# Attention and two mixture-of-experts layers: GpSimd splits the negated score maxima, weight loads placed between, and their transpose comes one score pair later

## The reference, cut to what matters

```python
x = x + _L0_ffn_ref(_L0_cond_ref(x, cond_1024, mask, ...), ...)
x = x + _L1_ffn_ref(_L1_cond_ref(x, cond_1024, L1_cond_weight), ...)
```

```python
scores = jnp.einsum('bhqd,bhkd->bhqk', q, k) / jnp.sqrt(jnp.float32(HDIM))
scores = jnp.where(causal[None, None], scores, jnp.float32(MASK_OUT))
scores = scores + mask
attn = jax.nn.softmax(scores, axis=-1)
out = jnp.einsum('bhqk,bhkd->bhqd', attn, v)
```

## Time and profile before

| What | us |
|---|---|
| three runs: lowest, median, highest | 392.42, 395.8, 398.46 |
| the profiled execution, its own time | 392.82 |
| its span, first to last instruction | 391.1 |
| mean granted clock of PE in it, share of full speed | 0.871 |
| attention stage in it (scores of group 0 to the last exponentials' use) | 35 to 156 |

### The profile page before, as it was taken

The page is one execution under the profiler, slowest core; times in us unless marked ns, Lnnn a source line. Parts: engine busy times, 40 slices in busy tenths (PEclk is TensorE's granted clock), DMA queues, the critical chain, the costliest instruction groups (busy, mean ns, idle before and its releaser), DMA issues.

```text
span 391.1 us, 8159 instructions
## 1 busy us (share of the span) xinstructions
PE 294.7 (75%) x2751; PEld 196.2 (50%) x2765; DVE 270.9 (69%) x717; ACT 184.4 (47%) x406; POOL 122.4 (31%) x161
## 2 busy tenths in 40 slices
PE   2747679999986798638988999999970748499800
PEld 1445334444433432327987867666640725277700
DVE  4396868888986563676997777777748686468503
ACT  7333056666752177502764445554445406167502
POOL 8304000101100057017055322222221077127760
PEclk9975689999998989655999999999995859789965
DMA  5679972345421024731278411110003011322114
GB/s 169 241 195 263 345 314 69 94 148 153 142 70 54 0 84 115 235 108 49 76 228 254 142 35 29 36 36 22 16 22 115 0 44 52 93 54 57 42 44 162
DMA packets 23238, 43.07 MB, mean 110 GB/s; under 512 B 4173, under 2 KB 13612, under 8 KB 23070
## 3 DMA queue, kind: packets, MB, share of 16 engines
q0 software_dynamic: 8336, 26.47, 20.3%
q1 hardware_dynamic: 13758, 13.38, 13.0%
q10 hardware_dynamic: 1104, 2.70, 1.8%
HBM read 26.99 MB, written 15.30 MB: 108 GB/s over the span
## 4 chain that ended last, share of the span: by engine, by line
PE 43%; DVE 20%; POOL 12%; DMA 9%; issue 9%; ACT 4%; SPq 1%; ACTq 1%; POOLq 0%; DVEq 0%
PE pair L1150 9%; POOL x_slots L685 6%; POOL y_rows L738 6%; DVE mA L1472 4%; PE bank L1171 4%; PE pair L979 3%; PE bank L1021 3%; PE pair L1120 3%; PE bank L999 3%; DMA xg<-x_slots 2%; DMA back<-y_rows 2%; PE bank L1160 2%; PE pair L981 2%; PE bank L1013 2%; DVE w_sb L1411 1%
## 5 line engine op out<-in xcount | busy, mean ns | idle before, releaser
L810 ACT ACTIVATE p_ring<-bank 128x512 f32<-128x512 f32 (+1 forms) x88 | 45.5, 566 | 33.7 <-PE bank L1002 33.5
L668 POOL DMA_DIRECT2D w_ring<-in_L_ffn_W_dram x24 | 18.4, 770 | 135.1 <-DVE w_sb L1411 116.3
L1472 DVE TENSOR_REDUCE mA<-pair 128x2 f32<-128x256 f32 (+3 forms) x64 | 50.8, 820 | 12.3 <-PE pair L981 12.1
L821 ACT ACTIVATE h<-pair,cols 128x128 f32<-128x128 f32 x108 | 30.8, 374 | 53.4 <-PE pair L1120 44.8
L685 POOL DMA_INDIRECT x_slots<-sent,slot x32 | 33.1, 1034 | 33.5 <-DVE slot L1721 17.2
L1150 PE MATMUL pair<-w_sb,h 128*128 x180 | 41.3, 379 | 0.0
L722 POOL DMA_INDIRECT y_rows<-y_sb,id_now x19 | 21.1, 1109 | 57.3 <-DVE y_sb L1616 42.6
L979 PE MATMUL pair<-kr,qr 128*128 128x128 bf16 (+3 forms) x122 | 33.7, 331 | 6.3 <-DVE mA L1472 5.4
L999 PE MATMUL bank<-qr,kr 128*128 128x384 bf16 (+3 forms) x120 | 31.2, 306 | 1.4 <-ACT p_ring L810 0.9
L1411 DVE SCALAR_TENSOR_TENSOR w_sb<-w_ring,w_sb 128x1024 f16<-128x1024 f32 x24 | 29.2, 1217 | 3.7 <-ACT w_sb L786 3.7
L821 ACT ACTIVATE h<-bank,cols 128x128 f32<-128x128 f32 x76 | 21.8, 368 | 15.0 <-PE bank L1135 7.6
(11 more groups left out here) (298 smaller groups left out, 625.7 us busy)
## 6 DMA issues: line engine op xcount, KB each, us to landing
w_ring<-in_L_ffn_W_dram POOLq DMA_DIRECT2D x24, 512.0 KB, 5.0
x_slots<-w_sb POOLq DMA_DIRECT2D x2, 2064.0 KB, 19.8
fc_sb<-in_L_ffn_c_fc_dram POOLq DMA_DIRECT2D x4, 512.0 KB, 5.4
cp_sb<-in_L_ffn_c_proj_dram POOLq DMA_DIRECT2D x4, 512.0 KB, 6.9
back<-y_rows SPq DMA_DIRECT2D x8, 256.0 KB, 3.2
kr<-k_rows SPq DMA_DIRECT2D x8, 204.0 KB
qr<-q_rows SPq DMA_DIRECT2D x8, 192.0 KB
x_slots<-w_sb ACTq DMA_DIRECT2D x1, 1290.0 KB, 6.4
```

What stands on the lines that cost most here:

```text
L810: act.activation(p_ring[:, w % P_RING, 0:width], bank(4 + v % 3)[:, 0:width], ACT.Exp).then_inc(exp_done, 1)
L821: ins = act.activation(to[:, c * P:(c + 1) * P], got[:, c * P:(c + 1) * P], ACT.Gelu, bias=cols[:, bass.ds(e * HC + (bias_row + c), 1)], s ...
L1472: dve.tensor_reduce(mA[:, b, t, g * G + 2 * hp:g * G + 2 * hp + 2], got[:, :, 0:(t + 1) * P], AX_X, ALU.max).then_inc(a_used, 1)
```

## The change

DVE's six small instructions for a group become one, `lowest`: it multiplies `mA` by -1 and takes the minimum with `simg`, which is now stored negated. The three parts are made by POOL, in the function `max_parts`, which waits for `neg_ready` and, from the second group on, for the `maxT` of the group before. POOL's loads of weights are placed between these: `max_parts(n + 1)` stands behind all loads whose slots are free once the low parts ahead of `maxT` of group n + 1 in the schedule are made. `maxT` stands behind the fifth score pair of a round instead of the fourth.

```diff
@@ a_pieces
-                out.insert(4 if n < groups else 0, ("maxT", n - 1))
+                out.insert(5 if n < groups else 0, ("maxT", n - 1))
@@ block.gpsimd
+            def max_parts(n):
+
+                pool.wait_ge(neg_ready, n + 1)
+                if n:
+                    pool.wait_ge(a_done, a_at[("maxT", n - 1)] + 1)
+                step(pool.tensor_copy(mp[:, :, 0, :], negm[:, :, :]))
+                pool.tensor_tensor(mr[:, :, :], negm[:, :, :], mp[:, :, 0, :], ALU.subtract)
+                step(pool.tensor_tensor(mp[:, :, 1, :], negm[:, :, :], mp[:, :, 0, :], ALU.subtract))
+                pool.tensor_tensor(mp[:, :, 2, :], mr[:, :, :], mp[:, :, 1, :], ALU.subtract).then_inc(m_parts, 1)
...
-            for n in range(W_RING, by_count[0]):
-                load_weights(n)
+            loaded = W_RING
+            for n in range(groups):
+                max_parts(n)
+                upto = max(loaded, W_RING + lows_before(("maxT", n + 1)) if n + 1 < groups else by_count[0])
+                for tile in range(loaded, upto):
+                    load_weights(tile)
+                loaded = upto
@@ block.vector
-            copy(simg[:, :, :, :].rearrange("p b t h -> p (b t h)"), bank(2)[:, 0:B * KC * H]
-                 ).then_inc(simg_ready, 1)
+            ts(simg[:, :, :, :].rearrange("p b t h -> p (b t h)"), bank(2)[:, 0:B * KC * H], -1.0, None, ALU.mult
+               ).then_inc(simg_ready, 1)
...
-            def maxima(n, first, last):
+            def lowest(n):
...
+                dve.wait_ge(a_used, a_at[("score", n, KC - 1, G // 2 - 1)] + 1)
+                if n:
+                    dve.wait_ge(m_parts, n)
+                dve.scalar_tensor_tensor(out=negm[:, :, :], in0=mA[:, b, :, mine], scalar=-1.0,
+                                         in1=simg[:, b, :, mine], op0=ALU.mult, op1=ALU.min).then_inc(neg_ready, 1)
...
-                    if n and t == 0:
-                        maxima(n - 1, 3 * hp, 3 * hp + 3)
+                    if n and (t, hp) == (0, 0):
+                        lowest(n - 1)
                     if (n, t, hp) == (groups - 1, KC - 1, G // 2 - 1):
-                        maxima(n, 0, 6)
+                        lowest(n)
```

More of the change, by code:

```diff
@@ L287, in build @@
             "fill_ready filled trimmed masked wqk_ready own_ready")
-        a_done, a_used, m_parts, s_done, exp_done, pv_done, o_ready, cnt_ready, slot_ready, tab_ready = sems(
-            "a_done a_used m_parts s_done exp_done pv_done o_ready cnt_ready slot_ready tab_ready")
+        a_done, a_used, neg_ready, m_parts, s_done, exp_done, pv_done, o_ready, cnt_ready, slot_ready, tab_ready = sems(
+            "a_done a_used neg_ready m_parts s_done exp_done pv_done o_ready cnt_ready slot_ready tab_ready")
         qk_in = [sem(f"qk_in{n}") for n in range(SLOTS)]
```

## The result

| | lowest | median | highest | runs |
|---|---|---|---|---|
| before, beside it | 392.42 | 397.13 | 398.81 | 4 |
| after | 411.00 | 415.07 | 418.06 | 4 |

The ratio is 1.0497, with an interval of 1.0313 to 1.0681: slower, as forecast, and 415.07 lies inside the range of 402 to 419. Ratios leave out the runs that lie over 1.5% above the fastest of their kernel, so this one is not that of the two medians, which is 1.045. The same kernel in a later session gave 415.25 and a ratio of 1.0452 (1.0382 to 1.0522). The profiled execution of after took 414.25 us (span 412.5, mean clock 0.857), 21.4 more than that of before.

What follows compares the result with a forecast made beforehand. PE was taken to bound the kernel, except 0.51 us a round waiting for DVE. Terms +0.2, +10.0, -2.0, +3.6 and +4.0 make +15.8 us: 408.6 on the profiled execution, 411.6 on the median; forecast 410, range 402 to 419.

Steps and rivals of the forecast that it cites:

- The mechanism: Rounds 3 to 6: PE's transpose must wait for low part, load and parts one after the other, some 3 us.
- The parts on POOL: A cast and three subtractions of 128x16 on POOL, taken as 0.9 us from a copy of that shape.
- The rival of slow parts: Parts take more than 0.9 us on POOL; at 2.4 us, +7.5 on top, 417.5; chance 0.12.
- The ports: POOL and DVE share ports; a low part could hold up the parts by 1.2 us, but adds nothing in middle rounds.
- The stalls: Rounds 3 to 6: PE stands still 3.1 us waiting for parts, +2.5 us a round, +10.0 together.
- The rival of hidden slack, half of it: PE or DVE has unseen slack, a stall costs 1.2 instead of 2.5; 399 to 404; chance 0.10.
- the clock, +4.0 for four stalls: Behind each stall of rounds 3 to 6 PE's clock halves for 3 us, costing 0 to 1.5, taken as 1.0.
- the rival of a clock that holds: The stalls come but PE keeps full clock: +11.8 us, 405 to 408; chance 0.20.
- The start, +0.2: Round 1: the copy of `mrow` comes behind the fifth reduction, so PE waits longer at 52.86; 0 to +0.4.
- Round 7 and the tail, -2.0: Round 7 and behind the last scores: DVE runs fewer small instructions, three pieces saving 2.0 us.
- The relief at the fourth score pair, 0.51 a round: Rounds 3 to 6: DVE's second reduction comes earlier, so PE gains its whole 0.51 us wait there.
- Round 8, +3.6: Group 7's parts stand behind the load issued at 138.51; the transpose comes at 140.2 instead of 136.66, +3.6 us.

Runs made afterwards that it cites:

- Kernel 1: The changed kernel with POOL making each group's parts ahead of the load it stood behind, for all groups; 395.32 us, ratio 0.9968 to before.
- kernel 3: The changed kernel with 44 useless PE products ahead of the transpose's wait in rounds 3 to 6; 409.39 us, ratio 1.0314 to before.
- kernel 4: The kernel before with only the transpose moved behind the fifth score pair; 399.05 us, ratio 1.0100 to before.
- kernel 5: The changed kernel once more, not edited, to know its spread; 415.25 us, ratio 1.0452 to before.
- kernel 2: The changed kernel with parts ahead of the tail's loads for group 7 only; 407.85 us, ratio 1.0260 to before.
- kernel 10: The same program as kernel 2, measured again in another session; 412.78 us, ratio 1.0415 to before.
- kernel 6: The changed kernel with parts ahead of the load for groups 2 to 6 only, group 7 unmended; 398.64 us, ratio 1.0046 to before.
- kernel 7: Kernel 1 with the transpose back behind the fourth score pair; 392.73 us, ratio 0.9920 to before.
- kernel 8: Kernel 7 with POOL issuing the two 2-MB slot-clearing transfers behind the parts of group 1; 390.14 us, ratio 0.9849 to before.

## Why the prediction was right, and where it was wrong

- **The mechanism: right.** The chain fourth score pair, low part, load, parts, transpose stands in the rows of after as forecast. The low part is at 2.83 us behind the round's first reduction (forecast 79.0 - 76.18 = 2.82), the load 1.51 behind it (1.52), the parts right behind the load's 0.72. Kernel 1 is the proof: with the load moved behind the parts, all of it goes, and the period falls below before's.
- **The parts on POOL: right within 0.1.** 0.98 us from the cast's start to the end at 87.60 (forecast 0.9), four instructions of 0.21 or 0.22. The rival of slow parts is out. The nearest shape (0.21) was the right row, not the nearest number of inputs (1.15). The rule of the Trainium skill, page "GPSIMD Engine Reference", section "Engine selection", that elementwise work with two inputs takes about twice as long there, does not hold at 16 elements a partition: 0.21 or 0.22 on POOL, 0.17 for DVE's small ones.
- **The ports: as the rule has it, at no cost.** In after the parts run while DVE has no low part, and nothing stretches them. Kernel 1 shows what such a meeting costs: 0.91 us on the cast, which ends with the low part. The rule of the Trainium skill, page "SBUF — State Buffer", section "Who interferes with whom", that the later of the two waits the earlier out, agrees with that. The forecast's remark on DVE's cast of 0.34 us stays untested: that cast has one input, which the rule as cited does not name, and no run takes it apart.
- **The stalls: right.** 2.85 us each where 3.1 were forecast, and +10.1 for the four rounds (kernel 3) where +10.0 were. The rival of hidden slack, half of it, is out, and so is the one that ends not slower.
- **The step that failed: the clock, +4.0 for four stalls.** It was taken from the one low stretch of before, 3 us long, and bounded at 1.5 each. In after PE was full behind every stall and the low stretches were longer: they cost up to 2.9 us each, and together 10.1 in the profiled execution and 7.2 in the next. The failed assumption is that a low stretch is as long as the one seen. The direction of the term was right, and the rival of a clock that holds is wrong in 13 of 16 rounds. The row that the forecast set against the fall, the wait of 1.62 us at 52.86, was a weak witness: there the clock had been 0.50 until 50.5 and had only just risen.
- **The start, +0.2: too small.** +1.15 in after, since PE reached the image key's products of group 0 sooner, found the rows of the maxima no sooner, and waited 3.30 us instead of 1.62, behind which the clock fell as well. The position costs 3.3 us there by itself (kernel 4), the relief of DVE takes some of it back. The forecast saw the wait and priced neither what a longer one does to the clock nor that its end is set by the transfer. The term also varies: after, kernel 5 and kernel 3 are one program up to there and come 1.15, 1.41 and 2.83 us later than before, as the low clock behind the wait lasts shorter or longer.
- **Round 7 and the tail, -2.0: -2.97.** DVE's shorter path gives 1.81 of it, up to PE's product that waited 2.22 us at 122.81 in the earlier trace rows. The other 1.16 is a clock: behind that wait it was 0.50, while in after the wait is 1.18 and the clock behind it 1.00:

```profile
142.38 0.30 PE L1068 MATMUL pair<-ident,on_sb 128*128 128x128 f32 x1 [1.18 <-DVE on_sb L1492]
```

```profile
142.40:145.40 3.00, 2.92 (x20) 1.37 (x20) 1.43 (x6) 1.82 (x3) 0.36 (x1) 1.00 0.55 175
```

The forecast counted what DVE saves and not the clock. The shorter wait is not enough to explain it, though. All nine executions of changed kernels have this same wait of 1.18 us. In after and kernels 5, 2 and 10, whose rounds 3 to 6 stand still for 2.9 us each, the clock held, and the stretch took 22.90 us every time. In kernels 3, 1, 6, 7 and 8, whose PE was kept at work in those rounds, it fell to 0.50 for about 3 us, and the stretch took 24.05 to 24.79. Why is open. It means that the stalled kernels got some 1.2 to 1.6 us back here that the others (kernels 3, 1 and 6) did not.
- **The relief at the fourth score pair, 0.51 a round: 0.30.** It shows only in the kernels without stalls in the rounds (1, 6, 7 and 8), since after's chain begins at that pair and its stalls hide the rest. PE's slack in the round went from 0.51 to 0.05, but its busy time grew from 11.13 to 11.29. Products that no longer wait begin in each other's shadow, so their modelled spans fill gaps that the forecast had counted as time to gain. That is argued from the windows, not shown by a run.
- **Round 8, +3.6: +3.62**, right in an execution with one long issue.

The sum on the profiled execution was 408.6 and came to 414.25; 6.2 of that is the four rounds, 0.95 the start, less 1.0 and 0.6 further on.

## What to carry to other kernels

When work moves to an engine that seems idle, look at what its queue already holds: here a load whose slot came free in mid-round stood ahead of four instructions of 0.2 us, and order alone made the difference between 415 and 395 us. Price a stall of a full TensorE not by its length only, but with a stretch at a lower clock behind it, as 13 of 16 rounds had here, and expect that part to vary from execution to execution. If filling the wait with useless products brings time back in the windows around it, the clock was a part of the loss; mending the order brings back both. Compare stretch by stretch: in kernel 3 the rounds gained 10.1 us and the whole only 3.9.

## What the runs showed that was not expected

- The clock's answer to equal stalls of 2.9 us is one of three amounts, about 0.1, 1.7 or 2.8 us, and not the same ones in two executions of one program. Behind waits of 1.62 and 1.99 us at 52 us the clock was full, behind waits of 2.72 and 3.30 at the same place it was not. But length alone does not decide: a wait of 1.18 us in the tail was followed by the full clock in four executions and by half of it in five.
- A small transfer took at least 1.7 times as long beside a large one. From SP's issue of group 0's rows of maxima to PE's start it took 6.17 us in before (46.69 to 52.86), 6.15 in after (46.37 to 52.52), 6.12 in kernel 4 and 6.16 in kernel 7, with the DMA share at 1.0 (the two 2-MB clearings). With the clearing moved away (kernel 8) it is at most 3.68 us (45.17 to 48.85), and the clearings themselves land in 10.3 us instead of kernel 7's 19.9. That constant delay is why a faster DVE only made PE wait longer there.
- One or two of the eight indirect issues on POOL take about 2 us where the others take 0.97, in before as in after. Executions with two such issues need 1.2 to 1.9 us more from the eleventh low part to `back` than those with one and no stall.
